# Two layer norms move from VectorE to ScalarE activations, and one copy of the values moves the other way

## The reference, cut to what matters

```python
x = x + conv_ref(ln_c(x))        # window attention, 12 heads of 16, windows of 64 tokens, relative position bias
t = to_tokens(x)
t = t + ffn_ref(ln_t(t))         # 9 experts of 192 -> 768 -> 192, top-1 routing; expert 0 is used by all tokens
def ln(v):                       # both norms, over the channels of one token; eps 1e-6 and 1e-5
    return (v - mean(v)) / sqrt(var(v) + eps)
```

## Time and profile before

| engine | busy us | share of the span | instructions |
|---|---|---|---|
| TensorE matmul (PE) | 278.2 | 89% | 3586 |
| VectorE (DVE) | 247.5 | 79% | 540 |
| ScalarE (ACT) | 189.2 | 61% | 410 |
| GpSimd (POOL) | 183.1 | 59% | 262 |

### The profile page before, as it was taken

How to read it: one execution, slowest core, us unless ns; L and a number is a source line. 1 busy time by engine, 2 the same in 40 slices (tenths; PEclk the granted TensorE clock), 3 DMA queues, 4 the chain that set the end, 5 groups by cost and what they waited for, 6 DMA issues and landing times.

```text
span 312.0 us, 9835 instructions
## 1 busy us (share of the span) xinstructions
PE 278.2 (89%) x3586; PEld 242.3 (78%) x3586; DVE 247.5 (79%) x540; ACT 189.2 (61%) x410; POOL 183.1 (59%) x262
## 2 busy tenths in 40 slices
PE   4995989899999798889799986899999999999993
PEld 4854657677777676667598886899999999999981
DVE  1847899999999889998945563988998898988463
ACT  1527587777777576877764544955465554554643
POOL 4247787888887769988953533000277676666400
PEclk9999899999999799999859999999999999999999
DMA  5614367524243423333330014112123333232066
GB/s 131 182 27 80 94 213 217 149 72 119 86 129 90 127 71 91 116 95 107 115 103 21 19 53 153 67 32 55 32 61 83 71 70 79 66 78 59 28 204 212
DMA packets 43105, 30.08 MB, mean 96 GB/s; under 512 B 20503, under 2 KB 42122, under 8 KB 43059
## 3 DMA queue, kind: packets, MB, share of 16 engines
q1 hardware_dynamic: 40691, 24.80, 29.4%
q0 software_dynamic: 1872, 4.36, 4.3%
q10 hardware_dynamic: 496, 0.31, 0.5%
HBM read 16.65 MB, written 8.91 MB: 82 GB/s over the span
## 4 chain that ended last, share of the span: by engine, by line
PE 63%; DVE 15%; issue 8%; ACT 6%; POOL 4%; DMA 1%; another core or an unknown queue 1%; DVEq 0%; POOLq 0%; ACTq 0%
PE p_s L1630 10%; PE p_t L1630 10%; PE p_qk L1659 10%; PE p_v L1659 8%; PE p_qk L1122 6%; DVE sc L895 4%; PE p_v L1135 4%; PE p_x L1204 3%; DVE kc L874 2%; PE p_t L1162 2%; PE p_n L1196 2%; PE p_s L1081 1%; ACT q L674 1%; DVE ka L874 1%; DVE on L925 1%
## 5 line engine op out<-in xcount | busy, mean ns | idle before, releaser
L1543 DVE TENSOR_TENSOR hp<-hf,hp 128x384 f16<-128x384 f32 x78 | 42.9, 556 | 26.2 <-ACT hf L1432 24.6
L1378 POOL DMA_INDIRECT routed_outputs<-yo,home x23 | 34.8, 1514 | 34.0 <-DVE yo L1558 32.8
L1429 ACT ACTIVATE hp<-p_t 128x384 f16<-128x384 f32 x38 | 18.7, 493 | 29.9 <-PE p_t L1630 27.0
L1429 ACT ACTIVATE hp<-p_s 128x384 f16<-128x384 f32 x40 | 19.8, 495 | 25.9 <-PE p_s L1630 25.8
L556 POOL TENSOR_SCALAR rstd<-mv 128x1 f32<-128x1 f32 x32 | 8.3, 258 | 39.4 <-DVE mv L864 28.7
L1122 PE MATMUL p_qk<-xnT,wT 96*128 96x128 f32 x192 | 25.4, 283 | 0.0
L1122 PEld LDWEIGHTS p_qk<-xnT,wT 96*128 96x128 f32 x192 | 23.3, 196 | 0.4
L1530 DVE COPY w1d<-w1s 128x3072 f16 x23 | 21.9, 954 | 0.6 <-issue 0.6
L1630 PE MATMUL p_t<-tokT,w1d 128*128 128x128 f16 (+1 forms) x360 | 22.4, 219 | 0.0
L550 POOL TENSOR_TENSOR sc<-sc,mx 128x768 f32<-128x768 f32 x15 | 22.1, 1474 | 0.1
L597 POOL DMA_INDIRECT sorted_tokens<-xhl,slot x16 | 16.9, 1054 | 7.8 <-DVE slot L987 4.7
(11 more groups left out here) (221 smaller groups left out, 780.8 us busy)
## 6 DMA issues: line engine op xcount, KB each, us to landing
w2stage<-in_L_ffn_W_dram SPq DMA_DIRECT2D x18, 288.0 KB, 3.2
w1stage<-in_L_ffn_W_dram SPq DMA_DIRECT2D x18, 192.0 KB
w1stage<-in_L_ffn_W_dram SPq DMA_DIRECT2D x36, 96.0 KB
xin<-in_x_dram SPq DMA_DIRECT2D x8, 192.0 KB, 3.5
routed_outputs<-void SPq DMA_DIRECT2D x1, 1536.0 KB, 7.8
w1d<-routed_outputs SPq DMA_DIRECT2D x8, 192.0 KB, 4.0
out_dram<-w2d SPq DMA_DIRECT2D x8, 192.0 KB, 2.8
sorted_tokens<-void SPq DMA_DIRECT2D x9, 128.0 KB
```

The lines of the kernel that those rows point to most:

```text
L1378: pool.indirect_dma_start(out=ys, out_offset=bass.IndirectOffsetOnAxis(ap=home[:, j:j + 1].bitcast(U32), axis=0), in_=yo[:, j % YB, :], in ...
L1429: act.activation(hp[:, n % 2, 0, HF * h:HF * h + HF, :], p_h[n % 2][h][:, 0:HF * T].rearrange("p (f t) -> p f t", f=HF), ACT.Gelu, scale=1 ...
L1543: dve.tensor_tensor(hp[:, n % 2, 1, HF * h:HF * h + HF, :], hf[:, n % 2, h, :].rearrange("p (f t) -> p f t", f=HF), hp[:, n % 2, 0, HF * h ...
```

## The change

`normed` and `xh` leave VectorE and become one ScalarE activation each: Identity(x * scale + bias) with scale = rstd and bias = -mean * rstd, both one number for each token. GpSimd makes the bias in a third instruction behind the power, in both norms. `keep_values_0` leaves ScalarE and becomes a VectorE copy in front of `keep_values_1`. In ScalarE's list `xh` and `xh_high` now stand in front of the first `split`, and `normed` behind it, in front of `keep_queries`.

```diff
+        shift = sb("shift", [128, 2, 2], F32)
...
-        ACT_PROGRAM = (("keep_x", 0), ("keep_attendedT", 5), ("keep_values_0", 1), ("split", 0),
-                       ("keep_queries", 1), ("keep_xhT", 7), ("exponentials", 3), ("xh_high", 6), ("split", 0),
+        ACT_PROGRAM = (("keep_x", 0), ("keep_attendedT", 5), ("xh", 6), ("xh_high", 6), ("split", 0), ("normed", 0),
+                       ("keep_queries", 1), ("keep_xhT", 7), ("exponentials", 3), ("split", 0),
                        ("keep_normedT", 0), ("weightsT_0", 3))
-        DVE_PROGRAM = (("statistics_1", 0), ("keep_values_1", 1), ("weightsT_1", 4),
-                       ("residual", 5), ("xh", 6), ("normed", 0), ("head_blocks", 1), ("add_bias", 2),
+        DVE_PROGRAM = (("statistics_1", 0), ("keep_values_0", 1), ("keep_values_1", 1), ("weightsT_1", 4),
+                       ("residual", 5), ("head_blocks", 1), ("add_bias", 2),
...
-            def inverse_deviation(t, ln, eps, ready, shifted, done):
+            def inverse_deviation(t, ln, eps, ready, shifted, done, minus_mean):
...
                 pool.tensor_tensor(r, r, minus_half[:, :], ALU.pow).then_inc(done, 1)
+                pool.wait_ge(done, t + 1)
+                pool.tensor_scalar(shift[:, ln, t % 2:t % 2 + 1], r, mv[:, ln, t % 2, 0:1], -1.0, ALU.mult, ALU.mult
+                                   ).then_inc(minus_mean, 1)
...
+            def normed(t):
+                act.wait_ge(shift1, t + 1)
+                if t >= 1:
+                    act.wait_ge(xnT_mm, t)
+                act.activation(xn[:, :], x2[:, t, :], ACT.Identity, bias=shift[:, 0, t % 2:t % 2 + 1],
+                               scale=rstd[:, 0, t % 2:t % 2 + 1]).then_inc(xn_ready, 1)
+
+            def xh(t):
+                act.wait_ge(shift2, t + 1)
+                if t >= 1:
+                    act.wait_ge(xh_hi, t)
+                    act.wait_ge(xh_lo, t)
+                act.activation(xhf[:, :], x2[:, t, :], ACT.Identity, bias=shift[:, 1, t % 2:t % 2 + 1],
+                               scale=rstd[:, 1, t % 2:t % 2 + 1]).then_inc(xh_ready, 1)
...
-                act.activation(v2[0:L, t % VB, :, :, 0, 0:HD], values(0), ACT.Copy).then_inc(v_kept[0], 1)
...
-                dve.scalar_tensor_tensor(out=xn[:, :], in0=x2[:, t, :], scalar=mv[:, 0, t % 2, 0:1],
-                                         in1=rstd[:, 0, t % 2:t % 2 + 1].to_broadcast([128, C]),
-                                         op0=ALU.subtract, op1=ALU.mult).then_inc(xn_ready, 1)
...
+                dve.tensor_copy(v2[0:L, t % VB, :, :, 0, 0:HD], values(0)).then_inc(v_kept[0], 1)
...
-                dve.scalar_tensor_tensor(out=xhf[:, :], in0=x2[:, t, :], scalar=mv[:, 1, t % 2, 0:1],
-                                         in1=rstd[:, 1, t % 2:t % 2 + 1].to_broadcast([128, C]),
-                                         op0=ALU.subtract, op1=ALU.mult).then_inc(xh_ready, 1)
```

More of the change, by code:

```diff
@@ L315, in attention @@
         rstd1 = sem("rstd1")
+        shift1 = sem("shift1")
+        shift2 = sem("shift2")
         xn_ready = sem("xn_ready")
@@ L562, in rstd_1 @@
                     pool.wait_ge(xn_ready, t - 1)
-                inverse_deviation(t, 0, 1e-6, mv1, rstd1a, rstd1)
+                inverse_deviation(t, 0, 1e-6, mv1, rstd1a, rstd1, shift1)
             def rstd_2(t):
@@ L567, in rstd_2 @@
                     pool.wait_ge(xh_ready, t - 1)
-                inverse_deviation(t, 1, 1e-5, mv2, rstd2a, rstd2)
+                inverse_deviation(t, 1, 1e-5, mv2, rstd2a, rstd2, shift2)
             def xh_low(t):
@@ L609, in gpsimd_part @@
                 if step == 2:
-                    pool.wait_ge(rstd1, 2)
+                    pool.wait_ge(shift1, 2)
                     zero_rows(range(NE))
@@ L754, in scalar_part @@
             keep_table()
+            normed(0)
             away_from_row(1)
@@ L759, in scalar_part @@
             keep_x(1)
-            keep_values_0(0)
             keep_queries(0)
             keep_bias()
+            normed(1)
             keep_normedT(1)
@@ L766, in scalar_part @@
                     small_weights()
-                stages(step, ACT_PROGRAM, (keep_x, keep_normedT, keep_queries, keep_values_0, exponentials, weightsT_0,
+                stages(step, ACT_PROGRAM, (keep_x, normed, xh, keep_normedT, keep_queries, exponentials, weightsT_0,
                                            keep_attendedT, xh_high, keep_xhT), split_high)
@@ L878, in head_blocks, with keep_values_0 @@
                 blk.then_inc(kbd_ready, 1)
+            def keep_values_0(t):
+                dve.wait_ge(v_mm, t + 1)
+                if t >= VB:
+                    dve.wait_ge(pv_mm, t - VB + 1)
+                if t == 0:
+                    dve.wait_ge(dve_consts, 11)
+                dve.tensor_copy(v2[0:L, t % VB, :, :, 0, 0:HD], values(0)).then_inc(v_kept[0], 1)
             def keep_values_1(t):
@@ L1011, in vector_part @@
             one_hots(0)
-            normed(0)
             away_from_row(1)
@@ L1016, in vector_part @@
             statistics_1(1)
+            keep_values_0(0)
             keep_values_1(0)
             head_blocks(0)
-            normed(1)
             tails()
@@ L1023, in vector_part @@
                     small_weights()
-                stages(step, DVE_PROGRAM, (statistics_1, normed, head_blocks, keep_values_1, add_bias, row_max,
-                                           weightsT_1, normalise, residual, xh, keep_logits, choose, slots), None)
+                stages(step, DVE_PROGRAM, (statistics_1, head_blocks, keep_values_0, keep_values_1, add_bias, row_max,
+                                           weightsT_1, normalise, residual, keep_logits, choose, slots), None)
                 if 0 <= step - DRAIN_STEP < DRAIN:
```

## The result

Twenty runs of the changed kernel have a median of 314.81 us (313.11 to 316.06), twenty of the kernel before beside them 313.87 us. The ratio is 1.0046, with an interval of 1.0024 to 1.0068: slightly slower, by less than the 1% that the prediction called no change, and above the 310.5 us forecast. The profiled execution took 314.53 us, its span is 312.8 us, 0.8 more than before.

What follows compares the result with a forecast made beforehand. VectorE was first suspect before the scatter, its norms delaying `ka`; GpSimd the bound in scatter steps. Terms -0.6 - 2.5 - 0.8 - 0.6 + 1.1 - 0.1 - 0.3 = -3.8 from 313.74 gave 309.9, median 310.5 us; range 307.0 to 315.5.

Steps and rivals of the forecast that it cites:

- Steps up to `on` at 53.92: First steps: `ka` no longer behind `xn`, but bias and subtraction 0.33 later; between 0 and -1.2 us, taken as -0.6.
- Five drained steps: Last steps of the first part: `xhf` no longer behind VectorE's expert work, TensorE mostly busy; -0.3 us.
- the period: Five steps from `on` at 53.92 to 94.56: 8.13 us each become 7.63, -2.5 us together.
- the two bounds that the sum names: In the five steps: GpSimd at 7.63 us, with TensorE's loop of 7.6 just under it.
- the bias: GpSimd's added instruction behind the power, in both norms: 0.32 us each, 0.65 a step.
- scatter steps: Three steps with a scatter, bound by GpSimd: 8.9 us each, 26.8 instead of 25.66, +1.1 us.
- The dear bias: Rival, chance 0.12: GpSimd's bias takes as long as the power, 0.68 us each; +4.3 us, 318.7 in the median.
- the two steps behind the scatter steps: One bias each, +0.3 us a step, but GpSimd's 0.76 wait for ScalarE's split goes; -0.1 us.
- the choosing step: Step to `on` at 103.50, where VectorE chooses experts: VectorE has room, GpSimd's late start stays in part; -0.8 us.
- The missing dip: Rival, chance 0.12: the clock stays up from 102 to 110 us, 1.7 us of stretching go; 308.8 us.
- Paid back through ScalarE: Rival, chance 0.20: in scatter steps `normed` waits for lagging GpSimd; six steps lose 0.3 more each, 1.8 us; 312.3.
- priced at nothing: ScalarE's added norms at 0.36 us each: 0.76 us of work fits the 0.81 idle in front of `q`.

Runs made afterwards that it cites:

- The unused bias: Kernel before, with GpSimd making both biases that nobody reads and the norms still on VectorE: 319.82 us, ratio 1.0224.
- the additional copy: Kernel before, with only the copy of the first half of the values moved from ScalarE to VectorE: 314.51 us, ratio 1.0030.
- the sixteen instructions: Kernel before, with 16 more ScalarE instructions that do nothing useful, in front of each `q`: 313.35 us, ratio 0.9976.
- that version: Kernel with only norm 2 on ScalarE, changed so that tiles 12 to 15 do it on VectorE without GpSimd's bias: 309.28 us, ratio 0.9865.

## Why the prediction was wrong

The mechanism of the middle was right, and it gave what was forecast. What failed lies at its two ends, together 4.1 us off: "Steps up to `on` at 53.92: I take -0.6" and "Five drained steps: -0.3".

- *Right: the period.* 7.62 us for 7.6, -2.5. `ka` behind `q`, VectorE idle in front of it, the split at 0.91. Of the two bounds that the sum names the order was the other way round: TensorE's loop through `q` gave the 7.63 from `on` to `on`, and GpSimd's step was 7.70, not 7.63. The reason is better known now: it was not VectorE's work that was late, but the end of GpSimd's instruction in front of `ka`. The unused bias lengthened the loop, the additional copy did not.
- *Right: the bias.* 0.35 for 0.32, scatter steps 8.99 for 8.9; the three to the subtraction cost +1.3 for +1.1. The dear bias is refuted.
- *Wrong: the steps up to `on` at 53.92* (-0.6; measured +1.95). 0.95 are the launch's. 1.02 are the order, a cost that the sum does not have: I followed the norm of tile 1 to its readers, but not what is queued behind it on ScalarE, `xnT`, `small_weights` and with them the statistics of tile 2. The forecast gain in the steps behind was 0: from the statistics of tile 2 to `on` it is 25.69 against 25.71.
- *Wrong: the drained steps* (-0.3; measured +1.2). The second norm on ScalarE in the last four tiles goes with a standstill of 1.3 to 1.4 us and one that is 1.3 longer. In all four kernels that have it there the fifth expert tile comes 6.05 to 6.15 us behind the fourth; in the eight without it, 4.7 to 4.8. Taking it away there, with its bias, gave 40.54 - 39.12 = 1.4 us. The step "`xhf` no longer stands behind VectorE's expert work" named a gain and no cost on ScalarE. Why ScalarE stands still is open: the list's length and GpSimd's bias are excluded, and the trace does not say what it waited for.
- *Wrong: the two steps behind the scatter steps* (-0.1; measured +0.3 by GpSimd's subtraction at 150.39 and 150.11). The wait of 0.76 for ScalarE went, but the second split, which now came earlier, waited 0.88 for the DMA of the scatter issued at 140.45: from the subtraction to the add behind the splits it is 4.24 us and was 4.27, so nothing was gained, and the one bias came on top. I named no wait that would be late next. In the step behind, the split at 152.53 took 1.52 and not 0.91; it starts beside VectorE's subtraction of the row maximum for the last tile, and that this is the reason was not tested.
- *Off in size: the choosing step* (-0.8; -0.4), since the statistics still reach GpSimd late (idle 1.39 for 1.83).
- *The missing dip,* a rival with 0.12, came in: 8.11 for 9.90, 1.8 us. But GpSimd was full by then and gave 0.9 back: 0.9 net. It can't be credited to the norms: the copy alone gave 8.74 without a dip, and the sixteen instructions 9.85 with one (granted clock 1.00 and 0.86 from 100 to 112 us).
- *Paid back through ScalarE:* `xn` waited 1.06 us for the bias in a scatter step, so the waits were real; yet the step stayed at 8.99, GpSimd's own. The rival's price was wrong.
- *ScalarE "priced at nothing":* the price held, though a term of it was wrong. A norm took 0.54, not 0.36, but `q` still started right behind TensorE's projection, 4.60 us behind `on` as before. That the larger norms just fitted is luck; the prediction did not know their size.

## What to carry to other kernels

When a step moves to another engine, read its unrolled list at the program's start and end too: an instruction that fits a gap of the steady loop can stand in front of the first tiles' work. A busy share of 95% does not make an engine the bound: adding 0.38 us of work to it, or 0.36 to the engine for which it may wait, tells which of them is. Of a change with a good middle, keep the middle and leave the ends as they were: that version had the lowest ratio here, 0.9865.

## What the runs showed of the hardware

- A norm of 128x192 on VectorE that starts beside GpSimd's subtraction or split ends behind it: 0.21 to 0.22 us with two SBUF tensors, 0.12 in the form with one. The statistics, which read one SBUF tensor, took 0.34 to 0.36 us in all 32 cases, beside GpSimd's work as well, and `ka`, which reads PSUM, 0.68 to 0.69 in all 16 tiles.
- A ScalarE activation with scale and bias per partition took 0.53 to 0.55 us on 128x192, a copy with no such operand 0.35. The same product of one number per partition took 0.27 us on GpSimd and 0.20 on VectorE.
- ScalarE stood still for 1.3 to 1.4 us in one place in four kernels and in none of the others, while TensorE had gone on to later work. The longer standstill, 2.8 to 2.9 us in the others, ends about 0.1 us behind matmuls of TensorE (start behind start) that come after gaps for which the trace has no releaser either (193.24 behind 193.16 in the changed kernel), so its cause may lie there. Neither was settled.
